# Attention in rounds of eleven key tiles, with 20 exponential buffers and a later weight fetch

## The reference

```python
h = _layernorm(x, ln1_g, ln1_b)
q = (h @ wq + bq).reshape(B, S, N_HEADS, dk)
k = (h @ wk + bk).reshape(B, S, N_HEADS, dk)
v = (h @ wv + bv).reshape(B, S, N_HEADS, dk)
scores = jnp.einsum('bqhd,bkhd->bhqk', q, k) / np.sqrt(dk).astype(np.float32)
attn = jax.nn.softmax(scores, axis=-1)
ctx = jnp.einsum('bhqk,bkhd->bqhd', attn, v).reshape(B, S, D)
x = x + ctx @ wo + bo
```

## Time and profile before

| what | us |
|---|---|
| median of three runs (1059.8 to 1062.15) | 1061.47 |
| the profiled execution | 1058.81 |
| its span, first to last instruction | 1056.6 |
| TensorE busy, share of the span | 827.3 (78%) |
| VectorE busy | 530.6 (50%) |
| ScalarE busy | 373.8 (35%) |
| attention: first slot to last value product | 118.6 to 378.9 |
| layer's output, router and scatter | 379 to 442 |
| eight experts of the first layer | 442 to 569 |

### The profile page before, as it was taken

The page is one execution under the profiler, slowest core; times in us unless marked ns, Lnnn a source line. Parts: engine busy times, 40 slices in busy tenths (PEclk is TensorE's granted clock), DMA queues, the critical chain, the costliest instruction groups (busy, mean ns, idle before and its releaser), DMA issues.

```text
span 1056.6 us, 12710 instructions
## 1 busy us (share of the span) xinstructions
PE 827.3 (78%) x3873; PEld 576.3 (55%) x3874; DVE 530.6 (50%) x1037; ACT 373.8 (35%) x757; POOL 132.3 (13%) x95
## 2 busy tenths in 40 slices
PE   5959799999999973199995459844499999999940
PEld 4846455555554342098895438723166666666630
DVE  4045777666666676188884559665022222222213
ACT  1004335555555642054551334030133333333310
POOL 2000000000000010724433200005400000000025
PEclk9989669999999997599998689975699999999975
DMA  7496803222231100414533635071100100000014
GB/s 251 162 341 238 192 1 73 66 66 49 64 69 34 28 18 0 150 62 155 193 112 122 262 114 184 1 318 68 53 30 30 30 30 30 30 30 30 25 37 131
DMA packets 54466, 102.40 MB, mean 97 GB/s; under 512 B 17978, under 2 KB 46220, under 8 KB 52764
## 3 DMA queue, kind: packets, MB, share of 16 engines
q1 hardware_dynamic: 51260, 94.16, 27.6%
q0 software_dynamic: 3168, 7.77, 2.3%
HBM read 72.16 MB, written 23.54 MB: 91 GB/s over the span
## 4 chain that ended last, share of the span: by engine, by line
PE 67%; DVE 14%; issue 6%; POOL 4%; DMA 4%; ACT 2%; SPq 0%; POOLq 0%; ACTq 0%; DVEq 0%
PE ps L1141 10%; PE ps L926 10%; PE ps L1159 10%; PE ps L906 6%; PE ps L857 5%; PE ps L918 5%; PE ps L1090 4%; PE ps L1150 2%; PE ps L1011 2%; PE ps L1012 2%; PE ps L1013 2%; DVE mx L1298 2%; DVE h_hi L1435 2%; PE ps L845 1%; POOL xs_d L660 1%
## 5 line engine op out<-in xcount | busy, mean ns | idle before, releaser
L1298 DVE TENSOR_REDUCE mx<-ps 128x1 f32<-128x452 f32 x264 | 148.0, 620 | 69.8 <-PE ps L906 68.5
L728 ACT ACTIVATE expo<-ps 128x452 f32<-128x452 f32 x264 | 124.3, 552 | 111.5 <-PE ps L918 110.5
L1141 PE MATMUL ps<-w_l,x1t_t 128*128 x232 | 109.3, 615 | 17.5 <-DVE x1t_t L1607 17.5
L926 PE MATMUL ps<-expo,v_st 128*64 128x452 f32 (+1 forms) x576 | 117.4, 529 | 0.0
L906 PE MATMUL ps<-k_st,q_st 96*128 96x452 f32 x264 | 111.5, 452 | 4.8 <-DMA k_st<-k_hi_d 4.6
L1159 PE MATMUL ps<-w_l,h 128*128 x464 | 106.7, 384 | 3.7 <-ACT h L828 3.7
L828 ACT ACT_TABLE_LOAD x29 | 37.2, 1283 | 203.6 <-PE ps L1150 203.6
L1159 PEld LDWEIGHTS ps<-w_l,h 128*128 128x128 f32 x464 | 89.4, 193 | 28.2 <-issue 17.4
L918 PE MATMUL ps<-q_st,k_st 98*128 98x452 f32 x264 | 96.8, 388 | 2.0 <-ACT expo L728 2.0
L1612 DVE COPY h1pre<-ps 128x1024 f32<-128x1024 f32 x29 | 35.5, 1225 | 116.9 <-PE ps L1141 116.9
L622 POOL TENSOR_TENSOR w_lo<-w_l,w_hi 128x2048 fp32r<-128x2048 f32 x8 | 46.8, 5846 | 348.1 <-ACT w_hi L750 348.1
(11 more groups left out here) (235 smaller groups left out, 1255.3 us busy)
## 6 DMA issues: line engine op xcount, KB each, us to landing
w_l<-w_l SPq DMA_DIRECT2D x8, 2053.0 KB, 8.8
w_l<-w_l SPq DMA_DIRECT2D x2, 8208.0 KB, 23.7
adj<-adj_t SPq DMA_DIRECT2D x22, 704.0 KB, 4.2
xs_d<-zeros SPq DMA_DIRECT2D x1, 3712.0 KB, 20.3
x1t<-xs_d SPq DMA_DIRECT2D x29, 128.0 KB, 2.1
ys_d<-y1t SPq DMA_DIRECT2D x29, 128.0 KB, 1.7
q_st<-q_hi_d SPq DMA_DIRECT2D x16, 176.0 KB, 3.2
k_st<-k_hi_d SPq DMA_DIRECT2D x16, 176.0 KB, 4.1
```

What stands on the lines that cost most here:

```text
L728: act.activation(expo[g % 8][:, :], ps[:, 3 + g % 3, 0:QC], ACT.Exp, scale=SCALE).then_inc(s_exp, 1)
L926: return pe.matmul(ps[at:at + 2 * DK, 6 + g // T % 2, lo:hi], v_st[h % 2][:, kt, :], expo[g % 8][:, lo:hi], start=kt < 2, stop=kt == T - 1 ...
L1141: mm = pe.matmul(ps[:, 2 + b, :], x1t_t[:, kt, :], w_l1[:, bass.ds(e, 1), at:at + 512].rearrange("p a n -> p (a n)"), start=kt == 0, stop= ...
L1298: dve.tensor_reduce(mx4[:, n // KB, n % KB:n % KB + 1], ps[:, i % 3, 0:KC], AX_X, ALU.max).then_inc(s_mx, 1)
```

## The change

Groups become whole thirds of 11 tiles, so that the order on TensorE is 11 scores of the next third with 11 or 12 slots between them, then 11 values. `expo` has 20 buffers in place of 8. The extra `AHEAD` slots all come with the first round, which now has a stretch of its own (`next_scores(-1)`: 8 slots, 11 scores). Values wait for the exponential of their own tile in place of the group's last. To make room, the second expert's weight buffer lies over `v_all` and `v_st`, and its fetch is issued at the end of attention, behind the last third's stores and a wait for the last value product. `load_max` of the next head moves ahead of the second third's store.

```diff
--- before.py
+++ after.py
@@ -26,7 +26,7 @@
 QB = 4
 THIRDS = 3
 COVER = THIRDS * QC
-PARTS = (4, 4, 3)
+EXPOS = 20
 NC4 = NP // QB
 KB = 3
 KC = 452
@@ -162,13 +162,13 @@
         adj0 = [place(f"adj0_{i}", [NP]) for i in range(3)]
 
         cursor[0] = arena
-        w_l0 = [place(f"w_l0_{i}", [WCOLS]) for i in range(2)]
+        w_l0 = [place("w_l0_0", [WCOLS])]
         attn_at = cursor[0]
         v_all = place("v_all", [T, D])
         v_st = [place(f"v_st{i}", [T, 2 * DK]) for i in range(2)]
         q_st = [place(f"q_st{i}", [NP], F32R) for i in range(3)]
         k_st = [place(f"k_st{i}", [NP], F32R) for i in range(3)]
-        expo = [place(f"expo{i}", [QC]) for i in range(8)]
+        expo = [place(f"expo{i}", [QC]) for i in range(EXPOS)]
         ctx_raw = [place(f"ctx_raw{i}", [QC]) for i in range(2)]
         den_even = place("den_even", [DT, COVER])
         den_odd = place("den_odd", [DT, COVER])
@@ -184,6 +184,7 @@
         assert cursor[0] <= offsets["ctx_raw0"]
 
         cursor[0] = attn_at
+        w_l0.append(place("w_l0_1", [WCOLS]))
         xs0 = [place(f"xs0_{i}", [CT, D]) for i in range(2)]
         w_hi = [place(f"w_hi{i}", [B1AT], F32R) for i in range(2)]
         w_lo = [place(f"w_lo{i}", [B1AT], F32R) for i in range(2)]
@@ -404,8 +405,7 @@
         block = ctx.enter_context(nc.Block())
 
 
-        GROUPS = [range(third * T + sum(PARTS[:n]), third * T + sum(PARTS[:n + 1]))
-                  for third in range(H * THIRDS) for n in range(len(PARTS))]
+        GROUPS = [range(n * T, (n + 1) * T) for n in range(H * THIRDS)]
 
 
         TURN = [(h + 1) * CHUNKS + h + min(2, (H - 1 - h) * CHUNKS) for h in range(H)]
@@ -420,7 +420,7 @@
 
         def slots_by(phase):
 
-            return min(SLOTS, FILL + -(-SLOTS * (phase + 1) // len(GROUPS)) + min(phase + 1, AHEAD))
+            return min(SLOTS, FILL + AHEAD + -(-SLOTS * (phase + 1) // len(GROUPS)))
 
         YT_AT = 3
 
@@ -455,8 +455,7 @@
                          zeros[:, None, :].to_broadcast([P, TILES1, D])).then_inc(s_zfill, 16)
 
             sp.wait_ge(s_g0_row, T)
-            for e in range(2):
-                sp.dma_start(w_l0[e][:, :], a["w_l0"][e]).then_inc(s_w0[e], 16)
+            sp.dma_start(w_l0[0][:, :], a["w_l0"][0]).then_inc(s_w0[0], 16)
 
             for n, (hi_d, lo_d, mt, c) in enumerate(qk_chunks):
                 there = (slice(mt * P, mt * P + P), slice(c * NC4, c * NC4 + NC4))
@@ -513,10 +512,12 @@
                     if h + 1 < H:
                         load_values((h + 1) % 2, h + 1)
                 store_third(h, 0)
-                store_third(h, 1)
                 if h + 1 < H:
                     load_max(h + 1)
+                store_third(h, 1)
             store_third(H - 1, 2)
+            sp.wait_ge(s_av, PRIMED + H * UNITS)
+            sp.dma_start(w_l0[1][:, :], a["w_l0"][1]).then_inc(s_w0[1], 16)
 
 
             def load_xs0(k, e):
@@ -723,9 +724,9 @@
             def exps(g):
 
                 act.wait_ge(s_s2, g + 1)
-                if g >= 8:
-                    act.wait_ge(s_av, PRIMED + g - 7)
-                act.activation(expo[g % 8][:, :], ps[:, 3 + g % 3, 0:QC], ACT.Exp, scale=SCALE).then_inc(s_exp, 1)
+                if g >= EXPOS:
+                    act.wait_ge(s_av, PRIMED + g - EXPOS + 1)
+                act.activation(expo[g % EXPOS][:, :], ps[:, 3 + g % 3, 0:QC], ACT.Exp, scale=SCALE).then_inc(s_exp, 1)
 
             def copy_third(n):
 
@@ -739,8 +740,8 @@
             for j, group in enumerate(GROUPS):
                 for g in group:
                     exps(g)
-                if j and j % len(PARTS) == 0:
-                    copy_third(j // len(PARTS) - 1)
+                if j:
+                    copy_third(j - 1)
             copy_third(H * THIRDS - 1)
 
             def weights_high(k, loaded):
@@ -923,7 +924,7 @@
 
                 h, kt = g // UNITS, g % T
                 at = 2 * DK * side
-                return pe.matmul(ps[at:at + 2 * DK, 6 + g // T % 2, lo:hi], v_st[h % 2][:, kt, :], expo[g % 8][:, lo:hi],
+                return pe.matmul(ps[at:at + 2 * DK, 6 + g // T % 2, lo:hi], v_st[h % 2][:, kt, :], expo[g % EXPOS][:, lo:hi],
                                  start=kt < 2, stop=kt == T - 1, skip_group_check=True)
 
             def group_values(group):
@@ -932,8 +933,8 @@
                     pe.wait_ge(s_v_st[first // UNITS % 2], first // UNITS // 2 * 16 + 16)
                 if first % T == 0 and first >= 2 * T:
                     pe.wait_ge(s_cr, PRIMED + first // T - 1)
-                pe.wait_ge(s_exp, PRIMED + group[-1] + 1)
                 for g in group:
+                    pe.wait_ge(s_exp, PRIMED + g + 1)
                     if g % T == T - 1:
                         values(g, 0, 0, QC // 2)
                         values(g, 1, QC // 2, QC).then_inc(s_av, 1)
@@ -945,16 +946,19 @@
             pe.wait_ge(s_vz, 7)
             for i in range(FILL):
                 fill_slot(i)
-            for g in GROUPS[0]:
-                scores(g)
-            for j, group in enumerate(GROUPS):
-                slots = list(range(slots_by(j - 1) if j else FILL, slots_by(j)))
-                for g in GROUPS[j + 1] if j + 1 < len(GROUPS) else ():
+            def next_scores(phase):
+
+                slots = list(range(slots_by(phase - 1) if phase >= 0 else FILL, slots_by(phase)))
+                for g in GROUPS[phase + 1] if phase + 1 < len(GROUPS) else ():
                     if slots:
                         fill_slot(slots.pop(0))
                     scores(g)
                 for i in slots:
                     fill_slot(i)
+
+            next_scores(-1)
+            for j, group in enumerate(GROUPS):
+                next_scores(j)
                 group_values(group)
```

## The result

The changed kernel takes 1070.26 us, median of eight runs (1068.32 to 1075.67), against 1061.6 for the kernel before on the same chips: ratio 1.0092, 95% interval 1.0077 to 1.0107, 8.7 us slower by the medians and 9.8 by the ratio. The forecast was 12.0 us slower, 1073.5.

What follows compares the result with a forecast made beforehand. TensorE, busy at full clock, was taken to bound attention. Attention's end moved to 388.3 (+9.4), the tail made it +12.0: 1058.81 + 12.0 = 1070.8, or 1073.5 on the median's footing; range some 1069 to 1079, down to 1066 with early clock.

Steps and rivals of the forecast that it cites:

- three signs by which it would be wrong: Thirds under 9.8 us, waits for VectorE that don't grow, or the clock leaving 1.00 between 165 and 380 us.
- Values in one piece: Value products of a third: each join saves 0.15 us, so two joins take them from 4.63 to 4.33 us.
- The added waits: One wait for each value tile in place of one a group: cost nothing, at most 2.6 us for 264.
- Scores and slots in one piece: Rounds 1 to 18: VectorE paces slots from slot 5 on; 5.56 us with eleven slots, 5.87 with twelve, 105.0 together.
- The forecast waits: In the long rounds, TensorE waits for VectorE's reductions before slots 5 to 10.
- The last rounds: Scoring in rounds 19 to 22: round 19 takes 6.4 us, three scores-only stretches 4.60 each, 13.8 together.
- The clock in the last rounds: Rival: clock halves in scoring stretches; four rounds without slots lose some 1.7 us each, about 7, giving 1081; chance 0.06.
- My argument against: Against a falling clock: the last thirds already had waits, with TensorE busy 4.49 of 5 us at granted 1.00.
- The beginning: Start of attention: round 0's values start at 157.6 us, their first 3.4 us at half clock, 1.7 us lost.
- The rival: Start of attention: dense scores alone raise the clock at about 145, first values at 154.0, total 1068; chance 0.22.
- The moved transfers: Second expert's later weight fetch, behind the last third's stores: costs nothing, at most 13.9 us if uncovered.
- The tail: End of attention: normalisation starts 6.21 us after the last third but one's values, at 390.3 against 378.29, +12.0 us.

Runs made afterwards that it cites:

- e2_old_groups: Changed kernel with groups of 4, 4 and 3 and their slots as before, all other parts of the change kept: 1060.13 us, ratio 0.9993 to the kernel before.
- e4_half_reduce_changed: Changed kernel with VectorE's row maxima over the first 226 of 452 columns of a slot: 1048.16 us, ratio 0.9882 to the kernel before.
- e8_again_look: Changed kernel again, no edit, to trace a quicker execution: 1072.48 us median of two, ratio 1.0114 to the kernel before; the traced execution took 1069.26 us.

## Why the prediction was right

The sign and the mechanism were right, and the main terms were nearly exact; two terms that had to do with the clock were wrong and went opposite ways. Of the three signs by which it would be wrong, one came: the clock left 1.00 between 165 and 380. In its order:

- **Values in one piece**, 4.33: measured 4.32. The added waits at nothing: ratio 0.9993 in e2_old_groups.
- **Scores and slots in one piece**: 5.56 forecast and 5.55 measured for eleven slots. The 18 stretches together: 337.91 - 155.10 - 18 x 4.32 = 105.0, forecast 105.0. e4_half_reduce_changed shows that it is VectorE's time, by making it shorter. The forecast waits are there too, 120 in place of 38.
- **The last rounds**: 4.60 a stretch. In the quick execution 377.46 - 368.51 - 4.35 = 4.60 at full clock; in the profiled one 4.81 to 4.89.
- **The clock in the last rounds**: I had it as a rival with 0.06 and a loss of 1.7 us a round. It came in the profiled execution: 6.13 + 5.79 + 5.57 + 5.47 - 4 x 4.32 = 5.7 us in the values, and with the stretches that fall into it (round 19's 7.00 in place of 6.4, three at 0.2 to 0.3 more) 7.1. My argument against was that the last thirds already had waits at a granted 1.00. There values follow after one such wait; in a long round eight scores in a row wait, each for 0.28 us at most. The step was an inference from single waits to a row of them. Round 19 was left out of it as well: its pause of 1.66 us for the turn stood in no row. The Trainium skill, "TensorE: Matmul & The Clock Gate", section "A second HAM failure mode: psum-queue depth-cycling", describes short idling between groups with a clock that goes up and down; these traces agree in that, with a granted clock that falls from 1.00 to 0.50 at about 359.6 and is back at 363 in the profiled execution.
- **The beginning**: "the first 3.4 us of values run at half rate" and values from 157.6 on. They began at 155.10 and took 4.32: 4.2 us too many. The clock rose between 148 and 149 in the middle of scores and slots. So values are not needed for it; that it had risen with the first values before I read as a cause. (The 3.4 us are no row's either: values at half clock are there from 146.73 to 149.94, 3.2 us.) From 142.60 on a score or a slot started every 0.376 us, and the rise came 5.4 us later. In e4_half_reduce_changed's trace scores start at 138.81, and the rise comes at 143.1, 4.3 us later, but slots alone, one every 0.41 us, had run there for 14 us at 0.50:

```profile
120.59 14.65 PE L907 MATMUL ps<-k_st,q_st 96*128 96x452 f32 x35 [4.51 <-DMA k_st<-k_hi_d]
...
121.00:135.00 14.00, 14.00 (x35) 9.60 (x34) 12.77 (x34) 0.00 (x0) 0.00 (x0) 0.50 0.68 148
```

  The rule of the same page of the Trainium skill, section "What's actually happening", that activity as such releases the throttle, agrees with the rise and not with these slots. What of the scores and slots together raises the clock stays open. The rival was right that values aren't needed, with first values at 154.0 forecast; its time for the rise ("about 145") was too early.
- **The moved transfers**, at nothing: the fetch is there 68 us ahead of its use.
- **The tail**: 6.2 us from the end of a third's values to its normalisation forecast, 391.20 - 386.79 = 4.4 measured, for the last of the four transfers landed in 2.0 us where it took 3.7. Why it lands sooner stays open.

12.0 - 4.2 + 7.1 - 1.8 = 13.1 us for the start of that normalisation, measured 391.20 - 378.29 = 12.9. That the forecast 12.0 is so near is luck: the three errors cancel. Against the median the sum is 3.2 us too high: in the quicker executions the clock falls less. In e8_again_look's, attention ends at 381.84 + 4.2 = 386.0, and 388.3 was forecast. The last 1.9 us of the profiled execution's 14.8 arise behind that point and were not followed: 1.0 ahead of the first expert's first product, which starts at 442.15 before and at 456.02 now, and 0.9 behind it.

## What to carry to other kernels

A ring of three buffers between a fast producer and a slower reader carries a burst only as long as the reader's lag fits into it; here four or five slots. Longer bursts ran at the reader's pace (0.536 us a slot), though VectorE was busy for 112 of 182 us only. So compare the reader's interval with the producer's in the burst, not over the round. Joining bursts saved a fixed cost at each join (0.15 us in the values here). Lay that against what each further slot costs, the reader's interval less the producer's (0.535 - 0.41 us here), and look also at what each engine does in the new long stretches: those in which TensorE only followed ScalarE were, here, the ones where the clock fell.

## What the runs showed of the hardware that I had not expected

- In rounds 20 to 22 the granted clock fell to half with TensorE never idle for longer than 0.28 us, 3.1 to 4.5 us after the first of the scores, which came 0.437 us apart. It did so in seven of nine such rounds, in three executions, and in none of six, in two executions, with work put between.
- While slots alone ran one every 0.535 us, the clock stayed at 0.50 for the 18 us of it, and also for 14 us with one every 0.41 us. It rose 4.3 and 5.4 us after scores and slots had begun to follow each other every 0.376 us.
- One and the same kernel differed by 3.6 us between two series of runs (1070.26 and 1073.89), each tighter than that for the most part. For an effect below half a per cent, only runs of one series are to be compared.
